# Rounding of the down weights moved from GpSimd to ScalarE, their stores to HBM set three pairs later in SyncE's order, the second layer's constants made in the second batch

## The chip, the cores and the metric

One core of one Trainium2 chip. The metric is the device time of one execution in microseconds, median of the runs.

## The reference

Two layers with residuals, x of shape (2, 1024, 256), all fp32:

```python
# layer 0: 8 experts and a shared one, F = 1024
g = einsum('bsd,edf->ebsf', h, Wg);  u = einsum('bsd,edf->ebsf', h, Wu)
expert_outs = einsum('ebsf,efd->ebsd', silu(g) * u, Wd)
expert_output = einsum('be,ebsd->bsd', gating_probs, expert_outs)
shared = (silu(h @ Sg) * (h @ Su)) @ Sd
x = x + (1 - sg) * expert_output + sg * shared
# layer 1: scores = tanh(x @ W1 + b1) @ v; per batch a mask (l<=j, l>=j or l!=j),
# p = softmax(where(mask, scores, -1e30)), x = x + (p @ x) / count(mask)
```

## The kernel before

**Work units.** The 9 experts (the shared one is the ninth) times 8 tiles of F give 72 *uses* of weights; two neighbouring uses are a *pair* (36 pairs). The groups i = 0 to 143 are batch 0's uses 0 to 71 and then batch 1's. Every fp32 matmul is made of three passes over a rounded part (hi) and a rest (lo), `three_pass`, L1477. Gate and up products use seven Strassen-like products per use instead of eight (`product`, L1482), so a use has 7 x 3 matmuls for gate and up and, in batch 0, 2 x 2 x 3 for the down product (`down`), each over 512 columns.

**Weights.** In batch 0 each weight is loaded raw, combined and split into hi and lo, used, and the split form is stored in HBM (`wq_kept` for gate and up, one use at a time; `wd_kept` for down, one pair at a time, with four sums of its tiles for batch 1). Batch 1 only fetches these.

- Gate/up of use n: GpSimd combines the raw tiles of a pair (`combine_pair`, L550 to L553), ScalarE rounds the hi (`round_w`, L792, issued three uses ahead), VectorE subtracts for the lo (`rest_w`, L1104). `wq` has three slots. `round_w(n)` waits until slot n % 3 is stored.
- Down of pair k: GpSimd does all: `split_d` (L564 adds zero to round, L567 subtracts), then `sums_d`: three sums (L580, L581, L582) in the raw buffer, their rounding (L584) and rest (L587). `raw_d` has two buffers, `wd` three slots.

**Order in each engine.** All orders are written out by hand. TensorE in use i (L1732 to L1764): p4(i), gate_start(i+1) (product 1), p5(i), down(0, i-2), gate_end(i+1) (product 2, which adds to what ScalarE's `seed` put down, and waits for it), p3(i), p7(i+1), p6(i+1), down(1, i-2). ScalarE in use i (L976 to L999): seed, gate_second, gate_first, round_h, keep_p7, round_h, keep_v, round_w; in uses 3 to 6 also batch 1's `round_x`. VectorE's loop L1369 to L1389 does batch 1's combinations and rests of x in uses 2 to 7.

SyncE issues all loads and stores of the loop in one order (L480 to L491):

```python
sp.wait_ge(gu_split, n + 1)
if n % PAIR == PAIR - 1 and m < NU // PAIR:
    load_gu(sp, m)
sp.dma_start(wq_kept[n], ...)
if n % PAIR == PAIR - 1:
    k = n // PAIR
    sp.wait_ge(td_split, k + 1)      # GpSimd's last rest of pair k, L587
    if m < NU // PAIR:
        load_d(sp, m)
    sp.dma_start(wd_kept[k], ...)
```

So the next use's store stands behind the last operation of GpSimd on the pair.

**Constants.** GpSimd makes the second layer's constants, flags and masks (63 small instructions, each waited for) between batch 0's uses: ahead of uses 13, 17, 21 and 25 (`EXTRA`, L669).

**Batch 1.** GpSimd has `sums_h(p)` alone (s3 L708, s1 L711, s2 L713, s4 L717), 35 times. ScalarE's odd group begins with `round_c("s3", p)`, which waits for L708, and has `seed` behind it. Batch 0's second layer is worked off in eight steps (`L1_STEP`) from group 74, two groups apart.

Of the kernel before, what the change touches and what calls it, by code (L numbers as in the profile page):

```python
# [6 lines left out]
F32 = mybir.dt.float32  # L7
# [25 lines left out]
def cond_resid_kernel(nc, x, fside, shared_gate, prompt_type, Wg, Wu, Wd, Sg, Su, Sd, W1, b1, v, out):  # L33
# [14 lines left out]
    RAWS = 2  # L48
    JB = BANK // D
# [20 lines left out]
    SPS = NU // PAIR - 1  # L70

# [6 lines left out]
    with ExitStack() as ctx:  # L78
# [52 lines left out]
        raw_d = place("raw_d", [P, RAWS, DN, P], F32, work_at + 8 * BANK * 4)  # L131
# [144 lines left out]
        staged_d = [sem(f"staged_d{s}") for s in range(RAWS)]  # L276
# [89 lines left out]
        L1_AT = end_of_b[0] + LAG + 1  # L366
# [81 lines left out]
        def load_d(queue, m):  # L448
            e, f = uses[m * PAIR]
            d = Wd[e] if e < E else Sd  # L450
            queue.dma_start(raw_d[:, m % RAWS, 0:PAIR * KD, :].rearrange("p (j k) d -> p j (k d)", k=KD),
                            d[f * P:(f + PAIR) * P, :].rearrange("(j p) d -> p j d", p=P)).then_inc(staged_d[m % RAWS], 16)
# [4 lines left out]
        @block.sync  # L457
        def _(sp):

            for i in range(0, NJ // PIECE, NT):  # L460
                load_x(sp, 0, i)
            load_x(sp, 0, NJ // PIECE - 1)
            load_w(sp, 0, Wg, (1,), slice(1, 3), staged_g[0])
            load_w(sp, 0, Wu, (1,), slice(0, 4, 3), staged_u[0])

            for i in range(NJ // PIECE):
                sp.wait_ge(x_loaded[0][i], 16)
            load_gu(sp, 1)
            sp.dma_start(probs[:], fside.unsqueeze(0).broadcast_to([P, B, E])).then_inc(gates_loaded, 16)
            sp.dma_start(sg[:], shared_gate.unsqueeze(0).broadcast_to([P, B])).then_inc(gates_loaded, 16)  # L470
            load_d(sp, 0)
            for i in range(NJ // PIECE):
                load_x(sp, 1, i)
            load_d(sp, 1)
            sp.dma_start(ptype_i[:], prompt_type.unsqueeze(0).broadcast_to([P, B])).then_inc(l1_loaded, 16)
            sp.dma_start(W1_sb[:, :, A:2 * A], W1.rearrange("(k p) a -> p k a", p=P)).then_inc(l1_loaded, 16)
            for t in range(NT):
                sp.dma_start(b1_sb[t * A:(t + 1) * A, :], b1.unsqueeze(1)).then_inc(l1_loaded, 16)
                sp.dma_start(v_sb[t * A:(t + 1) * A, t:t + 1], v.unsqueeze(1)).then_inc(l1_loaded, 16)
            for n in range(NU):  # L480
                m = n // PAIR + RAWS
                sp.wait_ge(gu_split, n + 1)
                if n % PAIR == PAIR - 1 and m < NU // PAIR:
                    load_gu(sp, m)
                sp.dma_start(wq_kept[n], wq[:, n % WR].bitcast(F32)).then_inc(wq_stored[n % WR], 16)
                if n % PAIR == PAIR - 1:
                    k = n // PAIR
                    sp.wait_ge(td_split, k + 1)
                    if m < NU // PAIR:
                        load_d(sp, m)  # L490
                    sp.dma_start(wd_kept[k], wd[:, k % DR].bitcast(F32)).then_inc(wd_stored[k % DR], 16)  # L491


            def fetch_d(p):

                k = SP0 + p
                if p < DR:
                    sp.wait_ge(wd_stored[k % DR], (SP0 - 1 - k % DR) // DR * 16 + 16)
                    sp.wait_ge(down_done[1], (k - DR + 1) * PAIR)
                else:  # L500
                    q = "s4" if (p - DR) % 2 else "a12"
                    sp.wait_ge(c_used[q], p - DR + 1)
                sp.dma_start(wd[:, k % DR].bitcast(F32), wd_kept[p]).then_inc(wd_fetched[k % DR], 16)

            for n in range(NU):
                i = NU + n
                sp.wait_ge(wq_stored[i % WR], (NU - 1 - i % WR) // WR * 16 + 16)
                sp.wait_ge(p_done[3], i - WR + 1)
                sp.dma_start(wq[:, i % WR].bitcast(F32), wq_kept[n]).then_inc(wq_fetched[i % WR], 16)
                if n % PAIR == 0 and n:  # L510
                    fetch_d(n // PAIR - 1)
            fetch_d(SPS)

            for b in range(B):
                for i in range(NJ // PIECE):
                    sp.wait_ge(out_done, b * NJ + (i + 1) * PIECE)
                    sp.dma_start(out_dram[b, i], x2[:, b, i * PIECE:(i + 1) * PIECE, :]).then_inc(stored, 16)
            sp.wait_ge(stored, 16 * B * NJ // PIECE)

        @block.gpsimd  # L520
        def _(pool):
# [33 lines left out]
            def split_d(n):  # L555
                s, j = n // PAIR % RAWS, n % PAIR
                if j == 0:
                    pool.wait_ge(staged_d[s], (n // PAIR // RAWS + 1) * 16)
                if n >= DR * PAIR:
                    pool.wait_ge(down_done[1], n - DR * PAIR + 1)  # L560
                    pool.wait_ge(wd_stored[n // PAIR % DR], n // PAIR // DR * 16)
                k, own = n // PAIR % DR, slice(j * KD, (j + 1) * KD)
                hi, lo = wd[:, k, 0, own, :], wd[:, k, 1, own, :]
                nc.gpsimd.tensor_tensor(hi, raw_d[:, s, own, :], zero[:, 0:1].unsqueeze(2).broadcast_to([P, KD, P]),  # L564
                                        ALU.add).then_inc(d_hi_done, 1)
                pool.wait_ge(d_hi_done, n + 1)
                nc.gpsimd.tensor_tensor(lo, raw_d[:, s, own, :], hi.bitcast(F32), ALU.subtract).then_inc(d_split, 1)  # L567
# [3 lines left out]
            def sums_d(k):  # L571


                def td_made(ins):
                    td_steps[0] += 1
                    ins.then_inc(td_step, 1)
                    pool.wait_ge(td_step, td_steps[0])

                w = raw_d[:, k % RAWS]
# [3 lines left out]
                hi, lo = wd[:, k % DR, 0, 4:DN, :], wd[:, k % DR, 1, 4:DN, :]  # L583
                nc.gpsimd.tensor_tensor(hi, w[:, 4:DN, :], zero[:, 0:1].unsqueeze(2).broadcast_to([P, DN - 4, P]),  # L584
                                        ALU.add).then_inc(td_hi_done, 1)
                pool.wait_ge(td_hi_done, k + 1)
                nc.gpsimd.tensor_tensor(lo, w[:, 4:DN, :], hi.bitcast(F32), ALU.subtract).then_inc(td_split, 1)  # L587
# [19 lines left out]
            def constants():  # L607
# [7 lines left out]
                const(nc.gpsimd.tensor_copy(to[:], to_i[:]))  # L615
                for at in LANES[1:]:
                    const(nc.gpsimd.tensor_scalar(lane[at:at + LANE, :], lane[at:at + LANE, :], -float(at), None, ALU.add))
                const(nc.gpsimd.tensor_scalar(lane_used[:], lane[:], float(NJ), None, ALU.is_lt))
                for m, compare in ((blk_before, ALU.is_gt), (blk_after, ALU.is_lt), (blk_same, ALU.is_equal)):
                    const(nc.gpsimd.tensor_scalar(m[:], to[:], lane[:, 0:1], lane_used[:, 0:1], compare, ALU.mult))  # L620
                const(nc.gpsimd.affine_select(out=eye[:], in_=ones[:, 0:NJ * NJ].rearrange("p (i j) -> p i j", j=NJ),
# [9 lines left out]
            def flags():  # L631
# [6 lines left out]
                const(nc.gpsimd.tensor_tensor(w_self[:], is_pre[:], is_post[:], ALU.add))  # L638
                for flag, w in ((f_before, w_before), (f_after, w_after), (f_self, w_self)):
# [5 lines left out]
            def masks(b):  # L645
# [7 lines left out]

                for m, one_way, other_way in ((blk_mask, blk_before, blk_after), (blk_mask_to, blk_after, blk_before)):
                    const(nc.gpsimd.tensor_scalar(m[:, b, :], one_way[:], w_before[:, one], None, ALU.mult))
                    const(nc.gpsimd.tensor_scalar(blk_part[:], other_way[:], w_after[:, one], None, ALU.mult))
                    const(nc.gpsimd.tensor_tensor(m[:, b, :], m[:, b, :], blk_part[:], ALU.add))
                for m in (mask[:, b, :], blk_mask[:, b, :], blk_mask_to[:, b, :]):
# [10 lines left out]
            EXTRA = {13: constants, 17: flags, 21: lambda: masks(0), 25: lambda: masks(1)}  # L669

            combine_pair(0)
            for n in range(NU):
                if n in EXTRA:
                    EXTRA[n]()
# [4 lines left out]
                split_d(n)  # L679
# [7 lines left out]
                if n == 3:  # L687
                    sums_d(0)
                if n % PAIR and n > 1:
                    sums_d(n // PAIR)  # L690
            assert steps[0] == CONST_STEPS
# [45 lines left out]
            for b in range(B):  # L737
# [3 lines left out]
                if b == 0:  # L741
                    for p in range(SPS):
                        sums_h(p)
                    join()
# [16 lines left out]
        def _(act):  # L761
# [21 lines left out]
            def round_w(n):  # L783

                act.wait_ge(t_step, 3 * (n // PAIR + 2 if n >= PAIR else n + 1))
                if n >= WR:
# [6 lines left out]
                                     ACT.Copy).then_inc(gu_hi_done, 1)  # L793

# [181 lines left out]
            for i in range(NU):  # L976
# [21 lines left out]
                for q in ROUND_X1.get(i, ()):  # L998
                    round_x(1, q)  # L999

# [62 lines left out]
        def _(dve):  # L1063
# [327 lines left out]
            def even(i, p):  # L1391
                second_gate(i)
                if i == L1_AT:
# [419 lines left out]
```

## Time and profile before

| | us |
|---|---|
| median of 3 runs | 1127.67 (1126.43 to 1129.34) |
| the profiled execution, its own time | 1127.99 |
| its span, first to last instruction | 1126.1 |
| TensorE busy in the span | 1104.9 (98%) |
| VectorE / ScalarE / GpSimd busy | 919.6 / 709.4 / 696.5 |

The profiled execution spends 1.9 us around its span. Batch 0's half ends at about 560 us. A sum of gains and losses is made against 1127.99, and what it gives is to be compared with the median of 1127.67, which is 0.3 us less.

### The profile page before, as it was taken

How to read it: one execution, taken by the hardware profiler on the slowest of the kernel's cores; microseconds unless marked ns; L12 is line 12 of the kernel's file. 1: busy time of each engine (PE TensorE's matmuls, PEld its weight loads, DVE VectorE, ACT ScalarE, POOL GpSimd, SP SyncE). 2: the span in 40 equal slices, each digit the busy share in tenths (PEclk: the TensorE clock that was granted, in tenths of full speed). 3: DMA queues.
4: the chain of work that ended last, by engine and by line, in shares of the span. 5: the costliest groups of instructions: out<-in, count | busy, mean ns of one | idle time of the engine just before them, and what ended most of it. 6: DMA issues, size and time to landing. Idle time of an engine off the chain costs nothing. (4 is left out here: it accounts for less than half of the span.)

```text
span 1126.1 us, 16076 instructions
## 1 busy us (share of the span) xinstructions
PE 1104.9 (98%) x4856; PEld 903.9 (80%) x4856; DVE 919.6 (82%) x1218; ACT 709.4 (63%) x1268; POOL 696.5 (62%) x666
## 2 busy tenths in 40 slices
PE   8799999999999999999999999999999999999988
PEld 6577888778888888888878887888888888888866
DVE  6698777788877877787668899888888898888875
ACT  6475666566666666666556666666666666666663
POOL 7799999999987777778324444444444444444451
PEclk9899999999999999999999999999999999999999
DMA  6666665487666666666545555555555555555512
GB/s 218 251 259 233 249 231 212 177 306 283 235 259 262 261 237 235 239 233 255 218 173 203 179 198 182 203 204 203 206 206 206 206 206 205 206 205 206 203 41 75
DMA packets 66484, 241.24 MB, mean 214 GB/s; under 512 B 6496, under 2 KB 38752, under 8 KB 57184
## 3 DMA queue, kind: packets, MB, share of 16 engines
q1 hardware_dynamic: 65584, 239.70, 57.6%
q8 instruction: 40, 0.66, 0.2%
q10 hardware_dynamic: 816, 0.52, 0.2%
q14 instruction: 44, 0.36, 0.1%
HBM read 134.29 MB, written 105.91 MB: 213 GB/s over the span
## 5 line engine op out<-in xcount | busy, mean ns | idle before, releaser
L811 ACT ACTIVATE silu<-g_ps 128x512 f32<-128x512 f32 x144 | 86.3, 599 | 180.1 <-PE g_ps L1480 180.1
L1478 PE MATMUL v_both<-xs_hi,wq 128*128 128x512 f32 x432 | 170.0, 393 | 3.3 <-DVE up L1146 2.6
L1479 PE MATMUL v_both<-xs_hi,wq 128*128 128x512 f32 x432 | 168.6, 390 | 0.0
L1480 PE MATMUL v_both<-xs_lo,wq 128*128 128x512 f32 x432 | 168.5, 390 | 0.0
L1141 DVE TENSOR_TENSOR gate<-e_ps,v_part 128x512 f32<-128x512 f32 x144 | 99.0, 687 | 66.4 <-PE e_ps L1480 66.2
L805 ACT ACTIVATE v_both<-g_ps 128x512 f32<-128x512 f32 x144 | 83.9, 583 | 101.7 <-PE g_ps L1480 101.4
L711 POOL TENSOR_TENSOR a<-a,a_own 128x512 f32<-128x512 f32 x35 | 56.1, 1604 | 137.4 <-DVE a_own L1173 137.4
L708 POOL TENSOR_TENSOR s<-a_own,a 128x512 f32<-128x512 f32 x35 | 56.3, 1610 | 131.0 <-DVE a_own L1192 131.0
L1478 PE MATMUL g_ps<-xs_hi,wq 128*128 128x512 f32 x288 | 113.0, 392 | 9.5 <-ACT v_both L805 9.5
L817 ACT ACTIVATE p_sb<-e_ps 128x512 f32<-128x512 f32 x144 | 86.2, 598 | 48.4 <-PE e_ps L1480 47.5
L1478 PE MATMUL e_ps<-xs_hi,wq 128*128 128x512 f32 x288 | 112.7, 391 | 0.4 <-ACT p_sb L817 0.4
L1480 PE MATMUL g_ps<-xs_lo,wq 128*128 128x512 f32 x288 | 112.4, 390 | 0.0
L1479 PE MATMUL e_ps<-xs_hi,wq 128*128 128x512 f32 x288 | 112.3, 390 | 0.0
L1480 PE MATMUL e_ps<-xs_lo,wq 128*128 128x512 f32 x288 | 112.3, 390 | 0.0
L1479 PE MATMUL g_ps<-xs_hi,wq 128*128 128x512 f32 x288 | 112.3, 390 | 0.0
L1478 PE MATMUL acc_of<-h_hi,wd 128*128 128x512 f32 x288 | 112.0, 389 | 0.0
L1479 PE MATMUL acc_of<-h_hi,wd 128*128 128x512 f32 x288 | 112.0, 389 | 0.0
L1480 PE MATMUL acc_of<-h_lo,wd 128*128 128x512 f32 x288 | 112.0, 389 | 0.0
L1146 DVE TENSOR_TENSOR up<-v_both,p_sb 128x512 f32<-128x512 f32 x144 | 98.7, 685 | 7.2 <-PE v_both L1480 3.3
L1104 DVE TENSOR_TENSOR wq<-raw,wq 128x896 fp32r<-128x896 f32 (+1 forms) x70 | 94.3, 1347 | 10.9 <-ACT wq L792 10.9
L1478 PEld LDWEIGHTS v_both<-xs_hi,wq 128*128 128x128 f32 x432 | 81.3, 188 | 24.9 <-DVE up L1146 7.3
L1201 DVE TENSOR_TENSOR a_lo<-a_own,a_hi 128x512 fp32r<-128x512 f32 x72 | 84.0, 1167 | 15.4 <-ACT a_hi L865 15.4
(233 smaller groups left out, 2883.5 us busy)
## 6 DMA issues: line engine op xcount, KB each, us to landing
wq_kept<-wq SPq DMA_DIRECT2D x72, 896.0 KB, 5.5
wq<-wq_kept SPq DMA_DIRECT2D x72, 896.0 KB, 4.5
wd_kept<-wd SPq DMA_DIRECT2D x36, 1024.0 KB, 5.4
wd<-wd_kept SPq DMA_DIRECT2D x36, 1024.0 KB, 6.1
raw_d<-in_L_cond_Wd SPq DMA_DIRECT2D x32, 256.0 KB, 3.1
raw<-in_L_cond_Wg SPq DMA_DIRECT2D x31, 256.0 KB, 2.7
raw<-in_L_cond_Wu SPq DMA_DIRECT2D x31, 256.0 KB, 3.5
out_x<-x SPq DMA_DIRECT2D x8, 256.0 KB, 2.1
```

The lines of the kernel that those rows point to most:

```text
L708: nc.gpsimd.tensor_tensor(s3[:], a_own[:], a21[p % 2][:], ALU.subtract).then_inc(sum_made["s3"], 1)
L711: nc.gpsimd.tensor_tensor(a21[p % 2][:], a21[p % 2][:], a_own[:], ALU.add).then_inc(sum_made["s1"], 1)
L805: nc.scalar.activation(v_ps[i % 2][:], g_ps[:], ACT.Copy).then_inc(seeded, 1)
L811: nc.scalar.activation(silu0[:, i % 2, :], g_ps[:], ACT.Silu).then_inc(silu0_done, 1)
L817: nc.scalar.activation(p7_sb[:], e_ps[:], ACT.Copy).then_inc(p7_copied, 1)
L1104: nc.vector.tensor_tensor(lo[:, part, :], raw[:, s, 1 + part.start:8, j * P:(j + 1) * P], hi[:, part, :].bitcast(F32), ALU.subtract).then_ ...
L1141: nc.vector.tensor_tensor(gate1[:], e_ps[:], v_part[:], ALU.add).then_inc(gate1_done, 1)
L1146: nc.vector.tensor_tensor(up1[:], v_ps[i % 2][:], p7_sb[:], ALU.add).then_inc(up1_done, 1)
L1201: nc.vector.tensor_tensor(lo, src[:], hi.bitcast(F32), ALU.subtract).then_inc(c_split[q], 1)
L1478: nc.tensor.matmul(ps, w_hi, a_hi, start=start, stop=False, skip_group_check=True)
L1479: nc.tensor.matmul(ps, w_lo, a_hi, start=False, stop=False, skip_group_check=True)
L1480: return nc.tensor.matmul(ps, w_hi, a_lo, start=False, stop=stop, skip_group_check=True)
```

## The change

Four things. (1) The hi parts of the down weights of pairs 1 to 35 are rounded by ScalarE (`round_d` at the end of even uses) and not by GpSimd; the hi parts of the sums of all pairs too (`round_td` at the end of odd uses). GpSimd keeps the subtractions (`rest_d`, `rest_td`) and the sums. (2) SyncE waits for `td_split` of pair k, loads down weights of pair k+3 and stores pair k only at use 2(k+3) (`KEEP = 3`); the last three pairs are stored between batch 1's first fetches. (3) `raw_d` has three buffers. (4) The constants are made in nine kinds of pieces after `sums_h(p)`, p = 1 to 11, and batch 0's second layer begins at group 104 in place of 74 (`L1_AT = NU + 32`).

```diff
+    RAWD = 3
+    KEEP = 3
-        L1_AT = end_of_b[0] + LAG + 1
+        ADD_AT = end_of_b[0] + LAG + 1
+        L1_AT = NU + 32
@@ SyncE
+            def keep_d(k):
+                sp.wait_ge(td_split, k + 1)
+                if k + RAWD < NU // PAIR:
+                    load_d(sp, k + RAWD)
+                sp.dma_start(wd_kept[k], wd[:, k % DR].bitcast(F32)).then_inc(wd_stored[k % DR], 16)
             for n in range(NU):
                 ...
-                if n % PAIR == PAIR - 1:
-                    k = n // PAIR
-                    sp.wait_ge(td_split, k + 1)
-                    if m < NU // PAIR:
-                        load_d(sp, m)
-                    sp.dma_start(wd_kept[k], ...)
+                if n == 1:
+                    load_d(sp, 2)
+                if n % PAIR == 0 and n // PAIR >= KEEP:
+                    keep_d(n // PAIR - KEEP)
             for n in range(NU):          # batch 1's fetches
+                k = (NU + n) // PAIR - KEEP
+                if n % PAIR == 0 and k < NU // PAIR:
+                    keep_d(k)
@@ GpSimd
+            def rest_d(k):
+                pool.wait_ge(d_hi_done, PAIR + k)
+                nc.gpsimd.tensor_tensor(wd[:, k % DR, 1, own, :], raw_d[k % RAWD][:, own, :],
+                                        wd[:, k % DR, 0, own, :].bitcast(F32), ALU.subtract)
+            def rest_td(k):
+                pool.wait_ge(td_hi_done, k + 1)
+                nc.gpsimd.tensor_tensor(... 4:DN ... subtract).then_inc(td_split, 1)
-            EXTRA = {13: constants, 17: flags, 21: lambda: masks(0), 25: lambda: masks(1)}
             combine_pair(0)
             for n in range(NU):
                 if n % PAIR == 0 and n + PAIR < NU:
                     combine_pair(n // PAIR + 1)
-                split_d(n)
-                if n % PAIR and n > 1:
-                    sums_d(n // PAIR)
+                if n < PAIR:
+                    split_d(n)
+                k = n // PAIR - 1
+                if n % PAIR == 0:
+                    if k >= 1:
+                        rest_d(k)
+                        rest_td(k - 1)
+                elif k >= 0:
+                    sums_d(k)
@@ GpSimd, batch 1, after sums_h(p)
+  p in 1..11: wait s4; edges, lanes, blanks, flags, biases, mask_of(0), block_masks(0),
+              mask_ends(0), mask_of(1), block_masks(1), mask_ends(1)
@@ ScalarE
+            def round_d(k):
+                act.wait_ge(staged_d[k % RAWD], (k // RAWD + 1) * 16)
+                if k >= DR:
+                    act.wait_ge(down_done[1], (k - DR + 1) * PAIR)
+                    act.wait_ge(wd_stored[k % DR], k // DR * 16)
+                nc.scalar.activation(wd[:, k % DR, 0, own, :], raw_d[k % RAWD][:, own, :], ACT.Copy)
+            def round_td(k):
+                act.wait_ge(td_step, 3 * (k + 1))
+                nc.scalar.activation(wd[:, k % DR, 0, 4:DN, :], raw_d[k % RAWD][:, 4:DN, :], ACT.Copy)
             for i in range(NU):
                 ...
+                if i % PAIR:
+                    round_td(i // PAIR)
+                elif i:
+                    round_d(i // PAIR)
```

## Rows read from the trace of the kernel before

**Rows 1.** Windows: busy us (count) of PE, PEld, DVE, ACT, POOL, then clock and DMA.

```profile
60.00:92.00 32.00, 30.65 (x133) 24.30 (x133) 31.44 (x37) 21.55 (x37) 30.36 (x28) 1.00 0.70 265
800.00:1060.00 260.00, 260.00 (x1149) 215.29 (x1148) 232.44 (x311) 171.63 (x311) 113.80 (x74) 1.00 0.56 201
```

**Rows 2.** Waits of TensorE: total us, times, longest.

```profile
PE g_ps L1478 <- ACT v_both L805: 9.5, 3, 7.8
PE v_both L1478 <- DVE up L1146: 2.6, 5, 0.8
```

**Rows 3.** Timeline of TensorE at 38 to 52 us: start, duration, [idle before].

```profile
38.53 0.39 PE L1480 MATMUL acc_of<-h_lo,wd 128*128 128x512 f32 x1
46.70 0.80 PE L1478 MATMUL g_ps<-xs_hi,wq 128*128 128x512 f32 x1 [7.78 <-ACT v_both L805]
51.86 0.39 PE L1478 MATMUL acc_of<-h_hi,wd 128*128 128x512 f32 x1
```

**Rows 4.** Timeline of TensorE at 223 to 229 us.

```profile
223.31 0.39 PE L1480 MATMUL acc_of<-h_lo,wd 128*128 128x512 f32 x1
225.17 0.50 PE L1478 MATMUL g_ps<-xs_hi,wq 128*128 128x512 f32 x1 [1.48 <-ACT v_both L805]
228.92 0.39 PE L1478 MATMUL acc_of<-h_hi,wd 128*128 128x512 f32 x1
```

**Rows 5.** Timeline of ScalarE: what stood before both gaps, and a regular seed.

```profile
45.21 0.95 ACT L792 ACTIVATE wq<-raw 128x896 fp32r<-128x896 f32 x1 [10.05 <-DMA wq_kept<-wq]
...
223.69 0.95 ACT L792 ACTIVATE wq<-raw 128x896 fp32r<-128x896 f32 x1 [3.82 <-POOL raw L553]
...
539.19 0.58 ACT L805 ACTIVATE v_both<-g_ps 128x512 f32<-128x512 f32 x1 [0.98 <-PE g_ps L1480]
```

**Rows 6.** Waits of SyncE's queue in the first 100 us.

```profile
SPq L451 <- POOL wd L587: 39.0, 4, 17.0
```

**Rows 7.** Timeline of SyncE's queue, first 60 us.

```profile
38.10 0.43 SPq L485 DMA_DIRECT2D wq_kept<-wq  x1
```

**Rows 8.** Groups of GpSimd, by form: busy us, mean ns, idle before.

```profile
L587 POOL TENSOR_TENSOR wd<-raw_d,wd 128x512 fp32r<-128x512 f32 x36 | 63.9, 1774 | 2.8
L584 POOL TENSOR_TENSOR wd<-raw_d,zero 128x512 fp32r<-128x512 f32 x36 | 42.0, 1167 | 2.8
L580 POOL TENSOR_TENSOR raw_d<-raw_d 128x256 f32<-128x256 f32 x36 | 35.2, 978 | 0.0
L581 POOL TENSOR_TENSOR raw_d<-raw_d 128x128 f32<-128x128 f32 x36 | 21.9, 607 | 2.8
L582 POOL TENSOR_TENSOR raw_d<-raw_d 128x128 f32<-128x128 f32 x36 | 20.9, 579 | 2.8
```

**Rows 9.** Groups of ScalarE, by form: a rounding from SBUF.

```profile
L835 ACT ACTIVATE h_hi<-h 128x512 fp32r<-128x512 f32 x72 | 45.2, 627 | 7.9 <-DVE h L1173 7.2
```

**Rows 10.** Groups of VectorE, by form: rests in batch 1's half.

```profile
L1201 DVE TENSOR_TENSOR a_lo<-a_own,a_hi 128x512 fp32r<-128x512 f32 x72 | 84.0, 1167 | 15.4 <-ACT a_hi L865 15.4
L1201 DVE TENSOR_TENSOR s_lo<-a,s_hi 128x512 fp32r<-128x512 f32 x71 | 48.5, 684 | 0.0
```

**Rows 11.** Timeline of GpSimd: first and last row of one mask's first six instructions.

```profile
204.24 0.78 POOL L647 TENSOR_SCALAR cnt<-pos,cnt_slope,cnt_rest 128x8 f32<-128x8 f32 x1
...
208.49 0.47 POOL L652 TENSOR_TENSOR mask<-mask,mask_part 128x128 f32<-128x128 f32 x1
```

**Rows 12.** Timeline of GpSimd, ScalarE and TensorE in a regular odd group of batch 1.

```profile
767.28 1.62 POOL L708 TENSOR_TENSOR s<-a_own,a 128x512 f32<-128x512 f32 x1 [3.44 <-DVE a_own L1192]
769.00 0.63 ACT L865 ACTIVATE s_hi<-s 128x512 fp32r<-128x512 f32 x1 [0.36 <-POOL s L708]
770.43 0.58 ACT L805 ACTIVATE v_both<-g_ps 128x512 f32<-128x512 f32 x1 [0.80 <-PE g_ps L1480]
771.59 0.39 PE L1478 MATMUL g_ps<-xs_hi,wq 128*128 128x512 f32 x1
```

More of the change, by code:

```diff
@@ L130, in cond_resid_kernel @@
         raw = place("raw", [P, RAWS, 8, PAIR * P], F32, work_at)
-        raw_d = place("raw_d", [P, RAWS, DN, P], F32, work_at + 8 * BANK * 4)
+        raw_d = [place(f"raw_d{n}", [P, DN, P], F32, work_at + at * BANK * 4) for n, at in enumerate((8, 10, 25))]
         blank = place("blank", [P, BANK], F32R, work_at + 12 * BANK * 4)
@@ L275, in cond_resid_kernel @@
         first_u = sem("first_u")
-        staged_d = [sem(f"staged_d{s}") for s in range(RAWS)]
+        staged_d = [sem(f"staged_d{s}") for s in range(RAWD)]
         wq_stored = [sem(f"wq_stored{s}") for s in range(WR)]
@@ L450, in load_d @@
             d = Wd[e] if e < E else Sd
-            queue.dma_start(raw_d[:, m % RAWS, 0:PAIR * KD, :].rearrange("p (j k) d -> p j (k d)", k=KD),
-                            d[f * P:(f + PAIR) * P, :].rearrange("(j p) d -> p j d", p=P)).then_inc(staged_d[m % RAWS], 16)
+            queue.dma_start(raw_d[m % RAWD][:, 0:PAIR * KD, :].rearrange("p (j k) d -> p j (k d)", k=KD),
+                            d[f * P:(f + PAIR) * P, :].rearrange("(j p) d -> p j d", p=P)).then_inc(staged_d[m % RAWD], 16)
         def load_x(queue, b, i):
@@ L485, in _ @@
                 sp.dma_start(wq_kept[n], wq[:, n % WR].bitcast(F32)).then_inc(wq_stored[n % WR], 16)
-                if n % PAIR == PAIR - 1:
-                    k = n // PAIR
-                    sp.wait_ge(td_split, k + 1)
-                    if m < NU // PAIR:
-                        load_d(sp, m)
-                    sp.dma_start(wd_kept[k], wd[:, k % DR].bitcast(F32)).then_inc(wd_stored[k % DR], 16)
+                if n == 1:
+                    load_d(sp, 2)
+                if n % PAIR == 0 and n // PAIR >= KEEP:
+                    keep_d(n // PAIR - KEEP)
             def fetch_d(p):
@@ L506, in _ @@
                 i = NU + n
+                k = i // PAIR - KEEP
+                if n % PAIR == 0 and k < NU // PAIR:
+                    keep_d(k)
                 sp.wait_ge(wq_stored[i % WR], (NU - 1 - i % WR) // WR * 16 + 16)
@@ L555, in split_d @@
             def split_d(n):
[L556 to L564, printed above, removed]
+                if n == 0:
+                    pool.wait_ge(staged_d[0], 16)
+                own = slice(n * KD, (n + 1) * KD)
+                hi, lo = wd[:, 0, 0, own, :], wd[:, 0, 1, own, :]
+                nc.gpsimd.tensor_tensor(hi, raw_d[0][:, own, :], zero[:, 0:1].unsqueeze(2).broadcast_to([P, KD, P]),
                                         ALU.add).then_inc(d_hi_done, 1)
                 pool.wait_ge(d_hi_done, n + 1)
-                nc.gpsimd.tensor_tensor(lo, raw_d[:, s, own, :], hi.bitcast(F32), ALU.subtract).then_inc(d_split, 1)
+                nc.gpsimd.tensor_tensor(lo, raw_d[0][:, own, :], hi.bitcast(F32), ALU.subtract).then_inc(d_split, 1)
+            def rest_d(k):
+                own = slice(0, PAIR * KD)
+                pool.wait_ge(d_hi_done, PAIR + k)
+                nc.gpsimd.tensor_tensor(wd[:, k % DR, 1, own, :], raw_d[k % RAWD][:, own, :],
+                                        wd[:, k % DR, 0, own, :].bitcast(F32), ALU.subtract).then_inc(d_split, PAIR)
             td_steps = [0]
@@ L577, in td_made @@
                     pool.wait_ge(td_step, td_steps[0])
-                w = raw_d[:, k % RAWS]
+                w = raw_d[k % RAWD]
                 td_made(nc.gpsimd.tensor_tensor(w[:, 4:6, :], w[:, 1:4:2, :], w[:, 0:2, :], ALU.subtract))
@@ L582, in sums_d @@
                 td_made(nc.gpsimd.tensor_tensor(w[:, 7, :], w[:, 2, :], w[:, 6, :], ALU.subtract))
-                hi, lo = wd[:, k % DR, 0, 4:DN, :], wd[:, k % DR, 1, 4:DN, :]
-                nc.gpsimd.tensor_tensor(hi, w[:, 4:DN, :], zero[:, 0:1].unsqueeze(2).broadcast_to([P, DN - 4, P]),
-                                        ALU.add).then_inc(td_hi_done, 1)
+            def rest_td(k):
                 pool.wait_ge(td_hi_done, k + 1)
-                nc.gpsimd.tensor_tensor(lo, w[:, 4:DN, :], hi.bitcast(F32), ALU.subtract).then_inc(td_split, 1)
+                nc.gpsimd.tensor_tensor(wd[:, k % DR, 1, 4:DN, :], raw_d[k % RAWD][:, 4:DN, :],
+                                        wd[:, k % DR, 0, 4:DN, :].bitcast(F32), ALU.subtract).then_inc(td_split, 1)
             def combine_pair(m):
@@ L605, in combine_pair, with edges @@
                 combine(s, slice(P, PAIR * P))
-            def constants():
+            def edges():
                 for m, sign in ((before, 1), (after, -1)):
@@ L615, in constants, with lanes @@
                 const(nc.gpsimd.tensor_copy(to[:], to_i[:]))
+            def lanes():
                 for at in LANES[1:]:
@@ L620, in constants, with blanks @@
                     const(nc.gpsimd.tensor_scalar(m[:], to[:], lane[:, 0:1], lane_used[:, 0:1], compare, ALU.mult))
+            def blanks():
                 const(nc.gpsimd.affine_select(out=eye[:], in_=ones[:, 0:NJ * NJ].rearrange("p (i j) -> p i j", j=NJ),
@@ L638, in flags, with biases @@
                 const(nc.gpsimd.tensor_tensor(w_self[:], is_pre[:], is_post[:], ALU.add))
+            def biases():
                 for flag, w in ((f_before, w_before), (f_after, w_after), (f_self, w_self)):
@@ L643, in flags, with mask_of @@
                 const(nc.gpsimd.tensor_tensor(cnt_rest[:], cnt_rest[:], w_self[:], ALU.add))
-            def masks(b):
+            def mask_of(b):
                 one = slice(b, b + 1)
@@ L652, in masks, with block_masks @@
                     const(nc.gpsimd.tensor_tensor(mask[:, b, :], mask[:, b, :], mask_part[:], ALU.add))
+            def block_masks(b):
+                one = slice(b, b + 1)
                 for m, one_way, other_way in ((blk_mask, blk_before, blk_after), (blk_mask_to, blk_after, blk_before)):
@@ L657, in masks, with mask_ends @@
                     const(nc.gpsimd.tensor_tensor(m[:, b, :], m[:, b, :], blk_part[:], ALU.add))
+            def mask_ends(b):
                 for m in (mask[:, b, :], blk_mask[:, b, :], blk_mask_to[:, b, :]):
@@ L667, in make_gates @@
                                         ALU.mult).then_inc(gate_step, 1)
-            EXTRA = {13: constants, 17: flags, 21: lambda: masks(0), 25: lambda: masks(1)}
             combine_pair(0)
             for n in range(NU):
-                if n in EXTRA:
-                    EXTRA[n]()
                 if n % PAIR == 0 and n + PAIR < NU:
@@ L686, in _ @@
                     nc.gpsimd.tensor_tensor(lo[:], raw[:, 1, 1:8, 0:P], hi[:].bitcast(F32), ALU.subtract).then_inc(gu_split, 1)
-                if n == 3:
-                    sums_d(0)
-                if n % PAIR and n > 1:
-                    sums_d(n // PAIR)
-            assert steps[0] == CONST_STEPS
+                k = n // PAIR - 1
+                if n % PAIR == 0:
+                    if k >= 1:
+                        rest_d(k)
+                    if k >= 1:
+                        rest_td(k - 1)
+                elif k >= 0:
+                    sums_d(k)
+            last = NU // PAIR - 1
+            rest_d(last)
+            rest_td(last - 1)
+            sums_d(last)
+            rest_td(last)
             def rest_carry(b, n):
@@ L743, in _ @@
                         sums_h(p)
+                        if p in range(1, 12):
+                            pool.wait_ge(sum_made["s4"], p + 1)
+                        if p == 1:
+                            edges()
+                        elif p == 2:
+                            lanes()
+                        elif p == 3:
+                            blanks()
+                        elif p == 4:
+                            flags()
+                        elif p == 5:
+                            biases()
+                        elif p in (6, 9):
+                            mask_of(p // 8)
+                        elif p in (7, 10):
+                            block_masks(p // 8)
+                        elif p in (8, 11):
+                            mask_ends(p // 11)
+                    assert steps[0] == CONST_STEPS
                     join()
@@ L793, in round_w @@
                                      ACT.Copy).then_inc(gu_hi_done, 1)
+            def round_d(k):
[3 more added lines that the diff above has]
+                    act.wait_ge(wd_stored[k % DR], k // DR * 16)
+                own = slice(0, PAIR * KD)
+                nc.scalar.activation(wd[:, k % DR, 0, own, :], raw_d[k % RAWD][:, own, :], ACT.Copy).then_inc(d_hi_done, 1)
+            def round_td(k):
+                act.wait_ge(td_step, 3 * (k + 1))
+                nc.scalar.activation(wd[:, k % DR, 0, 4:DN, :], raw_d[k % RAWD][:, 4:DN, :],
+                                     ACT.Copy).then_inc(td_hi_done, 1)
             def seed(i):
@@ L1392, in even @@
                 second_gate(i)
-                if i == L1_AT:
+                if i == ADD_AT:
                     add_acc(1, end_of_b[0])
```

## The prediction

> **What bounds the kernel now.** I read the windows first. TensorE has no gap in long stretches: 260.00 us busy of 260, with 1149 matmuls, so one takes 0.2263 us and a use of 33 matmuls 7.47 us [rows 1]. So a gain can only come from a gap or from slow matmuls, and less work on another engine is worth nothing by itself. Next, TensorE's waits. Besides the start and the tail there are two kinds: for ScalarE's seed, 9.5 us in three waits with one of 7.8, and for VectorE's `up`, 2.6 us in five [rows 2].
>
> Then the timeline at the two places. The long wait is followed by slow matmuls. In the code, twelve matmuls lie between the first one after the gap and the first one at normal pace, so from 38.53 to 51.86 us are 13 steps: 13 x 0.2263 = 2.94 us of work took 13.33 [rows 3]. The loss is 10.39 us: 7.9 idle and the rest from matmuls up to 0.80 us long, at the clock after the gap. At 223 us the same 13 steps took 5.61 us [rows 4]: loss 2.67.
>
> What made them? Ahead of the late seed stands `round_w`. The first waited 10.05 us for a store of `wq` [rows 5], issued only at 38.10 [rows 7]. In SyncE's order that store (use 2) stands behind the wait for GpSimd's last rest of pair 0, and SyncE's queue spent 39.0 us in four such waits, up to 17.0 each [rows 6]. The second `round_w` waited 3.82 us for GpSimd's own combination [rows 5], just after GpSimd had made a mask (rows of [rows 11] lie 15 us earlier). Both gaps are thus GpSimd being late, once through SyncE's order and once directly.
>
> **The change part by part.**
>
> *SyncE's order.* Store 2 no longer stands behind pair 0: it needs `gu_split` 3 only, which GpSimd gives in its first use. Store 3, the loads of pair 3 and all later ones move forward likewise; `load_d(2)` goes out at use 1. Each `keep_d(k)` asks for `td_split` of a pair three behind, which GpSimd ends about two uses earlier, so SyncE doesn't stand still in it, and what is queued behind it (load of down pair k+3, store of pair k, next `wq` stores) isn't late. The bytes are the same. Gain: 10.39 us.
>
> *GpSimd in batch 0.* It loses the rounding adds (1167 ns per pair at L584 and two of half size at L564) [rows 8] and all constants. That work is on no path of TensorE's by itself, but it is the lateness behind the second gap. Gain: 2.67 us. Cover gone would mean both gaps back, 13.06 us.
>
> *ScalarE in batch 0.* One more rounding of 128x512 per use: 0.63 us by the nearest row [rows 9]. It stands between `round_w` and the next seed, where ScalarE idles 0.98 us [rows 5]. How late may a seed be? The second gap tells: ScalarE was held 3.82 us and TensorE came 225.17 - 223.31 - 0.23 = 1.63 us late, so 2.2 us were absorbed. Cost in steady state 0.
>
> *Its waits.* `round_d(k)` waits for a load, a store and a down product; all were asked for well over a use before. `round_td(k)` waits for GpSimd's sums, and behind it stand seed, gates and TensorE. The chain from the end of `round_d(k)`: `rest_d` 1.77 (a 128x512 rest, like L587), `rest_td(k-1)` 1.77, sums 0.98 + 0.61 + 0.58 [rows 8], five hand-offs of 2.8/36 = 0.08: 6.1 us. `round_td(k)` is due one use after `round_d(k)` began: 7.47 - 0.63 = 6.8 us. Room 0.7, and 2.2 more before TensorE notices. Cost 0; lower bound 0; upper bound, if a chain in the first uses is late by a microsecond beyond that room, 1 each for two or three.
>
> *Third raw buffer, last three stores.* They only loosen waits; the fetches of batch 1 stand behind `keep_d(33)` to `keep_d(35)`, whose waits end before the fetch could go. Cost 0.
>
> *Uses 2 to 7.* Here VectorE has batch 1's x as well: 31.44 us busy of 32, TensorE 30.65 [rows 1]. The long gap let VectorE rest ahead of it. Without it, use 3 meets the same limit, so I add one more wait for `up` of the size of the others, with its slower first matmul: 0.8 us (bounds 0 and 2).
>
> *Constants in batch 1.* They lie in GpSimd's idle time between s4 and the next s3, 3.44 us [rows 12]. The longest piece is `mask_of`: 204.24 to 208.96, 4.7 us [rows 11], with the hand-offs 1.4 late. Then ScalarE rounds s3 at 770.4 instead of 769.00, seed starts 770.95 instead of 770.43 and ends 0.5 us later, at about 771.5; TensorE wants it at 771.59 [rows 12]. That is just in time, twice. A slower piece comes through one to one. VectorE can also be held up: a rest that meets GpSimd takes 1167 ns, one that doesn't 684 [rows 10]. I take 0.8 us for all eleven pieces, from below 0, from above 12 (rival D).
>
> The Trainium skill (SBUF — State Buffer, Who interferes with whom) says that a VectorE instruction with two SBUF inputs and a GpSimd one that reads SBUF exclude each other for the whole instruction, while ScalarE waits for nobody. This speaks for moving the rounding and against the new place of the constants; the pair 1167 and 684 ns agrees. By that rule the sum would stay as it is or go to rival D's.
>
> *Second layer at group 104.* Same work, same eight steps; the groups around it look the same. Cost 0.
>
> **Sum.** 1127.99 - 10.39 - 2.67 + 0.8 + 0.8 = 1116.5 us. The profiled execution is 0.3 above the median; I leave that in the range.
>
> **The rivals.**
>
> *A, as summed*: both gaps go. Its own range 1113.5 to 1119.5: bounds of the `up` waits (some of today's could shrink too, as GpSimd does less beside VectorE: 2.6 us at most) and 0 to 3 for the constants.
>
> *B, a part comes back*: ScalarE, VectorE and GpSimd are all near their limit in uses 1 to 8, and without the gap no one catches up. A late `round_td` or `rest_w` opens a new gap of 2 to 5 us, with slow matmuls behind it as in [rows 3]. For it: 31.44 of 32. Against it: 2.2 us of room for a seed. 1119.5 to 1123; I write 1121.
>
> *C, the first gap stays*: something besides the order holds `wq`'s store, as the DMA queues themselves. Against it: the row names the store, and it went out at 38.10. Only 2.67 gained: 1125.3.
>
> *D, no gain by contention in batch 1*: 63 instructions of GpSimd are put beside VectorE. If each lengthens one VectorE instruction by 1167 - 684 = 0.48 us, that is 30 us; VectorE idles 27.6 us of 260 [rows 1], some 1.6 per pair, so 11 pairs absorb 18 and 12 reach TensorE: 1128.5, that is no change. The rule quoted above would let this happen. Against it: most of the 63 are tiny, and they wait in turn.
>
> *E, slower*: the ScalarE and GpSimd chain. It is 6.1 us and may be 6.8 + 2.2 = 9.0. If contention stretches each GpSimd instruction by half, it is 9.2, which costs 0.2 us per pair, 7 us in 36, and only eats part of the gain. It decides against the change from 9.0 + 11.5/36 = 9.3 us on; at 9.5 us it is 36 x 0.5 = 18 us, so 1134.5. Against it: the 1774 ns of `L587` already hold today's contention.
>
> **How the numbers follow.** A 0.73, B 0.15, C 0.03, D 0.05, E 0.04. A change under 0.3% (3.4 us) is about what can't be told from none. A and B are faster, and a little of C and D: 0.90. Same 0.06, slower 0.04. The predicted time is A's. The range takes A and most of B: 1112.5 to 1121.5.
>
> **What would show it.** In the profile after: SyncE's `wq` store of use 2 goes out near 22 us, and its queue has no long wait for GpSimd; TensorE's wait of 7.8 us is gone and the granted clock stays full from 36 to 60 us; batch 1 begins about 13 us earlier. Per pair ScalarE has two 128x512 roundings into `wd`, and GpSimd's idle time before `rest_d` is filled with a wait for ScalarE. Around 610 to 730 us GpSimd's idle time before L708 shrinks, at `mask_of` to zero. Wrong would be: TensorE waiting for a seed behind `round_td` in each pair (E), new waits at 25 to 90 us (B), or `up` waits in batch 1's first third (D).

## The result and the profile after

The changed kernel takes 1122.72 us (median of 4 runs, 1122.43 to 1123.38), the kernel before 1128.2 in the same comparison. The ratio is 0.9954, with a 95% interval from 0.9936 to 0.9971: 5.5 us faster. The forecast was 1116.5, more than twice that gain, and the time lies above the upper end of the range (1121.5). The profiled execution took 1122.43 us with a span of 1120.7, against 1127.99 and 1126.1.

What was forecast of both gaps is there. In the waits of SyncE's queue in the first 100 us no line names GpSimd's last rest any more ([rows 6] had 39.0 us of it). The store of use 2 goes out at 22.01 us and not at 38.10 [rows 7]. These are the two with the largest totals, and a line of the queue's timeline:

```profile
SPq L445 <- DVE wq L1176: 30.7, 6, 7.6
SPq L498 <- DVE wq L1176: 27.9, 5, 7.4
```

```profile
22.01 0.34 SPq L498 DMA_DIRECT2D wq_kept<-wq  x1
```

The waits of TensorE's matmuls over the whole span leave nothing to explain a missing 6 us. These are the two with the largest totals; the first is the tail's:

```profile
PE acc_of L1550 <- issue: 2.4, 1, 2.4
PE v_both L1550 <- DVE up L1218: 1.9, 4, 0.6
```

The windows show it. These three rows are the same stretch of the kernel before, of the changed one and of experiment e1 (below), with the busy time of TensorE first and its count of matmuls in brackets:

```profile
60.00:560.00 500.00, 496.57 (x2182) 408.31 (x2182) 393.51 (x471) 311.79 (x533) 417.48 (x456) 1.00 0.64 245
```

```profile
60.00:560.00 500.00, 498.96 (x2171) 404.54 (x2170) 388.87 (x465) 342.00 (x593) 299.18 (x258) 1.00 0.65 242
```

```profile
60.00:560.00 500.00, 499.68 (x2203) 413.39 (x2202) 385.58 (x470) 349.52 (x599) 281.93 (x262) 1.00 0.66 246
```

TensorE is *busier* than before and does *fewer* matmuls in the 500 us: 2171 against 2182, although a gap was taken out. A matmul's row covers about 0.39 us while the next starts after 0.23, so a delay of up to 0.16 us is no idle time in the rows of the matmuls. One list of waits does name it, that of TensorE's weight loads (PEld). At 95 to 560 us, first before, then after:

```profile
PEld v_both L1478 <- DVE up L1146: 2.5, 8, 1.0
PEld v_both L1550 <- DVE up L1218: 9.9, 30, 0.3
```

Thirty waits in some 62 uses are one per pair. Their sum is what the weight loads waited, not what TensorE lost; for that I look at spacings, and take the start of ScalarE's `silu<-gate` of each use. In the changed kernel:

```profile
388.25 0.62 ACT L897 ACTIVATE silu<-gate 128x512 f32<-128x512 f32 x1
395.97 0.62 ACT L897 ACTIVATE silu<-gate 128x512 f32<-128x512 f32 x1
403.45 0.62 ACT L897 ACTIVATE silu<-gate 128x512 f32<-128x512 f32 x1
411.13 0.62 ACT L897 ACTIVATE silu<-gate 128x512 f32<-128x512 f32 x1
```

The distances are 7.72, 7.48, 7.68. I count a distance for the use or group in which it ends (the last of these is use 52's). Every use that should take 7.48 us does so when it is odd, and takes 7.68 to 7.73 when it is even. From use 10 to 70 this sums to 6.9 us. The same reading over both kernels gives the ledger of the difference (the changed kernel's lead over the kernel before, at the start of `silu<-gate` of that group):

| at group | lead, us | what lies between |
|---|---|---|
| 9 | 10.3 | first gap gone, uses 2 to 8 |
| 25 | 8.6 | eight even uses |
| 26 | 11.3 | second gap gone |
| 71 | 6.9 | even uses, less what before lost itself (about 13 was forecast here) |
| 104 | 15.2 | before has done the second layer of batch 0 here |
| 120 | 6.8 | the changed kernel does it here |
| 143 | 6.8 | |
| end of span | 5.4 | the tail |

The last step is new too. Both kernels wait some 2.4 us ahead of the last pair. In the changed one TensorE's clock then falls. Windows of the stretch behind that wait, first of before, then of after (the granted clock is the third number from the end):

```profile
1090.50:1094.50 4.00, 3.96 (x17) 3.10 (x18) 2.84 (x3) 3.99 (x13) 3.78 (x4) 1.00 0.02 4
```

```profile
1083.50:1087.50 4.00, 3.72 (x9) 3.00 (x10) 3.06 (x4) 3.99 (x12) 3.54 (x4) 0.57 0.01 4
```

Nine matmuls start there in place of 17, at a mean granted clock of 0.57: most of the stretch is at the lower of its two levels, 1.2 GHz.

### The profile page after: what moved, and what is told of

Its sections match the earlier page's. It is cut to its first block and busy times, and to the rows that moved or that the text cites. A ratio compares the mean times of both kernels' runs of the same rounds, so it can differ in the third digit from the quotient of the medians.

```text
span 1120.7 us, 15976 instructions
## 1 busy us (share of the span) xinstructions
PE 1109.0 (99%) x4856; PEld 901.3 (80%) x4856; DVE 921.3 (82%) x1218; ACT 746.8 (67%) x1339; POOL 603.5 (54%) x525
## 5 line engine op out<-in xcount | busy, mean ns | idle before, releaser
L584 POOL TENSOR_TENSOR wd<-raw_d,wd 128x512 fp32r<-128x512 f32 x35 | 46.3, 1324 | 190.8 <-ACT wd L855 190.8
L1176 DVE TENSOR_TENSOR wq<-raw,wq 128x896 fp32r<-128x896 f32 (+1 forms) x70 | 108.6, 1552 | 0.0
```

The costliest lines, as they stand in the source:

```text
L584: nc.gpsimd.tensor_tensor(wd[:, k % DR, 1, own, :], raw_d[k % RAWD][:, own, :], wd[:, k % DR, 0, own, :].bitcast(F32), ALU.subtract).then_ ...
L1176: nc.vector.tensor_tensor(lo[:, part, :], raw[:, s, 1 + part.start:8, j * P:(j + 1) * P], hi[:, part, :].bitcast(F32), ALU.subtract).then_ ...
```

## The experiments

**Who makes even uses slow.** Three timelines of the changed kernel around 403 us, first VectorE's, then GpSimd's, then TensorE's:

```profile
402.89 2.00 DVE L1176 TENSOR_TENSOR wq<-raw,wq 128x896 fp32r<-128x896 f32 x1
404.82 0.68 DVE L1218 TENSOR_TENSOR up<-v_both,p_sb 128x512 f32<-128x512 f32 x1
```

```profile
402.66 1.29 POOL L584 TENSOR_TENSOR wd<-raw_d,wd 128x512 fp32r<-128x512 f32 x1 [5.51 <-ACT wd L855]
403.89 2.15 POOL L604 TENSOR_TENSOR wd<-raw_d,wd 128x512 fp32r<-128x512 f32 x1
```

```profile
405.25 0.39 PE L1552 MATMUL g_ps<-xs_lo,wq 128*128 128x512 f32 x1
405.55 0.50 PE L1550 MATMUL v_both<-xs_hi,wq 128*128 128x512 f32 x1
405.89 0.40 PE L1551 MATMUL v_both<-xs_hi,wq 128*128 128x512 f32 x1
```

ScalarE's `round_d` ends (L855) and releases `rest_d` at 402.66, 0.23 us before VectorE's `rest_w` starts. This takes 2.00 us; `up` behind it is late, and TensorE's p3 starts 0.30 us after its predecessor, with a first step of 0.34. Both are 0.23 normally. The theory T is that these two instructions meet once in every pair, and that this makes the distance up to the even use longer. The rival R1 is that ScalarE's added rounding does it.

*e1: the two kept apart.*

```diff
             def rest_d(k):
                 pool.wait_ge(d_hi_done, PAIR + k)
+                if PAIR * k + 3 < NU:
+                    pool.wait_ge(gu_split, PAIR * k + 4)
```

> The changed kernel, but GpSimd's rest_d(k) also waits for VectorE's rest_w of use 2k+3 (gu_split 2k+4), so the two no longer run side by side; ScalarE's work and order are untouched. Theory T (in every even use of batch 0 rest_w, 2.0 us beside rest_d, makes VectorE's up late and TensorE loses 0.2 us): ScalarE's silu<-gate again follows itself at 7.48 us in even uses, rest_w falls to about 1.2 us in them, 33 x 0.2 = 7 us gained on the changed kernel's 1122.7: about 1116 (1114.5 to 1118). Rival R1 (ScalarE's added rounding in front of the seed costs the 0.2): unchanged, 1122 to 1124. Rival R2 (delaying rest_d makes the chain to round_td late): slower than 1123.

Measured 1113.47 us (1113.28 to 1115.09), ratio to before 0.9874 (0.9861 to 0.9888): 9.2 us less than the changed kernel. All uses from 10 to 71 take 7.48 us. A line on one source line (count, then shortest, median and longest ns) for `rest_w` at 95 to 560 us, first in the changed kernel, then in e1:

```profile
L1176 DVE TENSOR_TENSOR wq<-raw,wq x59: 1082/2003/2009, 99.3 to 539.5; 128x896 fp32r<-128x896 f32 x59
```

```profile
L1178 DVE TENSOR_TENSOR wq<-raw,wq x59: 1081/1084/1419, 98.0 to 531.8; 128x896 fp32r<-128x896 f32 x59
```

T holds and the rivals fall: ScalarE does the same work, and one more wait on GpSimd makes the kernel faster. By the profiled executions it is 8.9 us, of which 7.5 are there at group 143: 1.0 by use 9 and 6.9 in the even uses, less 0.4 at groups 93 and 94. The other 1.4 are the tail's clock, below. The time is below the range given for T, which had neither the tail nor the first uses in it. In the other use of each pair `rest_w` takes 1.41 us in e1, beside GpSimd's combination, and this costs nothing.

*e2: the subtractions replaced by memsets.*

```diff
-                nc.gpsimd.tensor_tensor(wd[..., 1, own, :], raw_d[...], wd[..., 0, own, :], ALU.subtract)
+                nc.gpsimd.memset(wd[:, k % DR, 1, own, :].bitcast(F32), 0.0)
                 # and the same in rest_td
```

> The changed kernel with rest_d and rest_td as memsets: the lo parts of the down weights of pairs 1 to 35 and of all their sums are left out (zero), so GpSimd reads nothing there and is quicker. ScalarE's work, its waits and all transfers stay. T: no 0.2 us per even use, about 1116, rest_w of even uses under 1.4 us. R1 (ScalarE) or R3 (the transfers' traffic): even uses stay at 7.68, 1122 to 1124.

Measured 1113.96 us. Uses from 10 on take 7.48 us, and `rest_w` 1163 ns in the mean. In the even uses it runs beside two memsets, which stand where the subtractions stood (VectorE's timeline, then GpSimd's):

```profile
397.09 1.08 DVE L1174 TENSOR_TENSOR wq<-raw,wq 128x896 fp32r<-128x896 f32 x1
```

```profile
396.84 0.53 POOL L584 MEMSET wd<- 128x512 f32 x1 [7.01 <-ACT wd L853]
397.30 0.53 POOL L603 MEMSET wd<- 128x512 f32 x1
```

This too ends R1, and the rival that the transfers do it (all of them are there): the delay needs GpSimd's subtractions at that moment. The memsets don't read, and they are shorter as well (0.53 us); but `rest_w` isn't even delayed to the end of the memset that was running when it began. The Trainium skill (SBUF — State Buffer, Who interferes with whom) has the lock that fits: a VectorE instruction with two SBUF inputs and a GpSimd one that reads SBUF, not one that only writes it, meet in it, and the second to issue waits for the whole of the first. The trace agrees within 0.15 us: at 402.89 `rest_w` had 1.06 us to wait for the end of `rest_d` and took 0.92 longer than alone, and GpSimd's next subtraction ended 1.15 us after `rest_w`, where one of this size takes 1.29 undisturbed.

*e3: the rounding back on GpSimd.* `split_d` and `sums_d` as in the kernel before (with three raw buffers), ScalarE without `round_d` and `round_td`; order and constants as changed.

> The changed kernel with the rounding back on GpSimd (new SyncE order, three raw buffers and constants in batch 1 are kept; ScalarE has nothing added). T: GpSimd's operations are no longer tied to ScalarE's round_d and fall on rest_w in no fixed place; both gaps of before stay away, so 1128.2 - 13 + 1 = about 1116 (1114 to 1118). If instead the new place of stores and loads, or any collision with GpSimd, costs the 0.2 us per even use, it stays at 1122 or above.

Measured 1121.1 us: the forecast missed by 5. The start is one cause. Without the first gap GpSimd, with 12 us of work per pair and a late begin, falls behind in uses 3 to 5 (10.79 and 9.28 us for two of them), and `silu<-gate` of use 9 is 5.3 us behind e1's. The other: GpSimd is tied again, to the store of `wd`, and lengthens *odd* uses by 0.04 to 0.13 us, 2.3 us in all; `rest_w` takes some 1.85 us there, once per pair. Lines of its waits, GpSimd's at 100 to 540 us and ScalarE's at 20 to 60:

```profile
POOL wd L578 <- DMA wd_kept<-wd: 78.1, 29, 4.4
```

```profile
ACT wq L831 <- POOL raw L567: 3.4, 1, 3.4
```

So moving the rounding to ScalarE is worth 5.3 + 2.3 us where `rest_d` is kept off `rest_w` (e1). Where it isn't, as in the changed kernel, it is worth nothing: 1122.7 against e3's 1121.1 by the medians, 1122.4 against 1122.3 in the profiled executions, which both have the low clock in the tail.

*e4: SyncE's order, with the third raw buffer and the later second layer.* As e3, constants back ahead of uses 13, 17, 21 and 25. These three are not told apart.

> As e3, and the constants back ahead of uses 13, 17, 21 and 25 of batch 0: of the change only SyncE's order, the third raw buffer and the later second layer are left. T: the first gap is gone (10.1 us), and a gap of up to 3 us may be left behind the masks: 1117 to 1119.5. Rival: with three buffers and the later stores GpSimd has more run-ahead, the second gap is gone too, and it equals e3.

Measured 1128.04 us, ratio 1.0 (0.9991 to 1.0009). The order takes 6.5 us out by use 9 and most of it is given back: gaps at uses 22, 23 and 26 behind the masks (11.41, 8.46 and 9.91 us for 7.48, 7.3 in all, against 2.9 in the kernel before), and the small delays of e3. In the profiled execution, the fastest of ten, 1.9 us are left; the medians show nothing. At 160 to 240 us ScalarE's `round_w` waited twice for GpSimd's combination, up to 4.9 us:

```profile
ACT wq L830 <- POOL raw L567: 8.3, 2, 4.9
```

I read it so: with the gap gone, TensorE reaches the masks sooner, and GpSimd's lateness, which the gap had covered, is seen there.

*e5: only the constants back in batch 0*, with ScalarE rounding.

> The changed kernel with the constants, flags and masks back ahead of uses 13, 17, 21 and 25 of batch 0; ScalarE's rounding and SyncE's order stay. Theory: GpSimd has some 5.5 us of idle time per pair there, but its place is tied to ScalarE's round_d; the 8 to 9 us of constants and of each mask come in front of a combination or a rest, are late by 3 to 4 us, of which about 2.9 us are absorbed: gaps of 0.5 to 3 us three times. Against it, 0.4 us less in batch 1 (groups 87 and 93): 1124 to 1128. Rival: GpSimd's idle time hides all of them: 1122.3, and the move of the constants was worth nothing with the rounding on ScalarE.

Measured 1143.41 us, ratio 1.0142 (1.0128 to 1.0155): 20.7 us over the changed kernel. The sign was right, the size four times the most that I gave (5.3). The four blocks cost 6.0 + 1.7, 3.2 less 1.1, 7.3 and 7.4 us. GpSimd's timeline at the first block (its first and last instruction), and then ScalarE's:

```profile
102.36 0.74 POOL L627 TENSOR_SCALAR_AFFINE_SELECT before<-ones 128x128 f32<-128x128 f32 x1
...
110.14 0.19 POOL L651 CAST pos<-pos_i 128x8 f32<-128x8 int32 x1
```

```profile
112.23 0.63 ACT L859 ACTIVATE wd<-raw_d 128x512 fp32r<-128x512 f32 x1 [6.23 <-POOL raw_d L600]
```

The 8 us stand between `rest_td` and the sums that `round_td` waits for, so nearly all of them are late, and GpSimd's idle time of 5.5 us comes after, not before. Rival E of the prediction, the ScalarE and GpSimd chain, is real as soon as anything is put into it. The move of the constants isn't a matter of 2.7 us: it is worth 6.9 us with the rounding on GpSimd (e4 to e3) and 20.7 with it on ScalarE.

**The tail.** *e6: matmuls in the wait.*

```diff
                 k, done = SP0 + SPS, {}
+                for _ in range(8):
+                    nc.tensor.matmul(e_ps[:], xs_hi[1][:, 0, 0:P], xs_hi[1][:, 0, :], start=True, stop=True, ...)
```

> The changed kernel with eight matmuls of 128x512 (their result is read by nobody) in TensorE's wait of 2.35 us ahead of the last pair. Theory: the profile of the changed kernel has 8 matmuls at 0.43 us behind this wait (the clock fell), as before has not; with TensorE busy the clock stays, 8 x 0.2 = 1.4 us gained: 1121.3. The fillers are 1.8 us and end before the wait does. Rival: the low clock there was this one execution's only, and the median stays at 1122.7, or is later by the part of the fillers that doesn't fit.

Measured 1121.35 us (1120.77 to 1121.54), 1.4 below, as forecast. From group 143 to the end of the span e6 takes 41.4 us and the changed kernel 42.8, so the gain is where it should be. TensorE's timeline of e6 has the fillers in the wait, and the last pair at full pace:

```profile
1081.58 1.98 PE L1645 MATMUL e_ps<-xs_hi 128*128 128x512 f32 x8
1084.12 0.47 PE L1550 MATMUL acc_of<-a_hi,wd 128*128 128x512 f32 x1 [0.57 <-issue]
1084.43 0.40 PE L1551 MATMUL acc_of<-a_hi,wd 128*128 128x512 f32 x1
```

*e7: e1 with the fillers.*

> e1_rest_after_rest_w with the same eight matmuls as in e6. Its profiled execution ran the last pair at full clock, but its four times lie between 1113.28 and 1115.09. Theory: the scatter is the tail's clock; with the fillers all lie at 1113.3 or 0.3 below, none above 1114. Rival: no effect on median or spread.

Measured 1113.49 us (1113.10 to 1113.92), none above 1114, though not all within 0.3 of 1113.3. The median is e1's: by its mean granted clock (0.998 and not 1.000) e1 had the low clock in one of its four times only, 1115.09. That the fillers narrow the scatter agrees with the theory but four times are few.

**The order's distance.** *e8: e1 with `KEEP = 2`.*

> e1_rest_after_rest_w with KEEP = 2: each down pair is stored and the next raw pair loaded one pair earlier in SyncE's order. Theory: at its place td_split of that pair comes about half a use after SyncE gets there (GpSimd ends rest_td(k) behind rest_d(k+1)), so SyncE stands for some microseconds per pair and what is behind it (the store of the next wq, the next gate and up load) goes out later; wq's stores have over a use of slack, so 1113.5 to 1115. Rival: the order of before was bad only because of uses 0 to 3, and at KEEP = 2 the start has a gap again: 1116 or more.

Measured 1126.71 us, outside the theory's range. For batch 0 the theory held: the late stores cost nothing (use 70 is reached 0.95 us earlier than in e1). The start has no gap, so the rival's reason is wrong as well. The loss is at the transition, which neither named. ScalarE's timeline, SyncE's queue there, and TensorE's wait at 540 to 575 us:

```profile
555.97 0.58 ACT L875 ACTIVATE v_both<-g_ps 128x512 f32<-128x512 f32 x1 [11.39 <-PE g_ps L1554]
```

```profile
547.26 0.32 SPq L491 DMA_DIRECT2D wd_kept<-wd  x1
547.69 1.34 SPq L523 DMA_DIRECT2D wq<-wq_kept  x2
```

```profile
PE g_ps L1552 <- DMA wq<-wq_kept: 10.5, 2, 9.1
```

With `KEEP = 2` the store of pair 34, which waits for GpSimd, stands ahead of batch 1's first fetch of `wq`; that goes out only at 547.69, and TensorE waits for it.

*e9: the same, the last two stores at e1's places.*

```diff
+    KEEP = 2
+                if n in (2, 4):
+                    keep_d(NU // PAIR - 3 + n // 2)
```

> e8 lost its time in one place: after use 70 ScalarE's silu<-gate is 17.56 us behind the last instead of 7.48, since keep_d(34) stood in front of batch 1's first fetch of wq. Here KEEP = 2 in batch 0's loop, and the last two pairs are stored where e1 stores them, ahead of the fetches of uses 74 and 76. Theory: that gap (some 12.9 us with what follows it) is gone, and what e8 had gained over e1 by use 70 (0.95 us) stays: 1112.6 (1112 to 1113.5). Rival: KEEP = 2 leaves SyncE so late at the transition that a part comes back: 1114 to 1120.

Measured 1113.53 us (1112.91 to 1115.34), just above the theory's range. The gap at the transition is gone, 13 us, but no more than e1 came of it: e8's lead over e1 in use 9 was 0.96 us, e9's is 0.43 and turns into -0.4 by use 23. `KEEP` 2 or 3 makes no difference that these runs can tell.

*e10: e9 with the fillers, and `mask_of` in two pieces.*

> e9 with the fillers of e6 and with mask_of cut in two pieces of some 2.4 us, after p = 6 and 7 and after p = 10 and 11, so that GpSimd has ended each before the next s3 is due. Theory: groups 87 and 93 (8.23 and 8.26 us in e1 for 7.48, of which the next group gave back half) lose nothing: 0.8 us less than e9, 1111.8, and no run above 1112.5. Rival: more GpSimd pieces collide with VectorE in other groups and it equals e9.

Measured 1112.94 us (1112.03 to 1113.17), ratio to before 0.9862 (0.9847 to 0.9876). Groups 87 and 93 take 7.44 and 7.48 us, and group 143 comes 1.1 us earlier than in e9, with a start 0.35 us later. Of the 1.1 us, 0.8 come after group 72, as the theory had it for the masks. By medians e10 is 0.6 below e9, and 1.1 above the 1111.8 that I gave; three of its four times are above 1112.5. It beats both kernels. Its four times are all below e1's four, but the intervals of the ratios overlap, so I don't call it faster than e1.

## Why the prediction was wrong

*The two gaps (-10.39 and -2.67).* Right. The lead at use 9 is 10.3 us, with the cost of uses 2 to 7 in it (-10.39 + 0.8 was forecast), and the second gap gives 11.3 - 8.6 = 2.7. That SyncE's order *alone* would bring the first of them, as the part on it says with "Gain: 10.39", is wrong: e4 has 6.5 us by use 9, and 1.9 at the end of its profiled execution, 0.1 by the medians.

*The step that failed: "Cost in steady state 0" for the rounding on ScalarE.* I weighed ScalarE's queue (0.98 us idle before the seed, 2.2 us of room) and the chain to `round_td`, and both held: e1 and e2 leave ScalarE's work as it is. In the changed kernel's timeline the seed still has 0.47 us of idle before it, and GpSimd waits for ScalarE, not ScalarE for GpSimd:

```profile
POOL wd L584 <- ACT wd L855: 190.8, 35, 9.2
```

What I didn't ask is *when* `rest_d` would now run. A wait on ScalarE's `round_d` fixes its start to a point in TensorE's cycle, and 0.2 us later `rest_w` starts there, with `up` and p3 behind it. Before, GpSimd ran free and met `rest_w` at any phase; its median there was 1275 ns, and TensorE's weight loads waited for `up` 8 times and not 30 in the same stretch. The cost was 6.9 us in 31 even uses. I had the mechanism in hand, with its rule, and applied it to the constants in batch 1 (rival D) only; my text even read it as "speaks for moving the rounding".

*Constants in batch 1 (+0.8).* Small, as forecast, and half of it. `mask_of` makes groups 87 and 93 late by 0.8 and 0.25 us, and the next group gives back 0.42 and 0.25: 0.4 in all. GpSimd's timeline of the first, and the s3 that it pushes:

```profile
662.70 0.35 POOL L671 TENSOR_SCALAR cnt<-pos,cnt_slope,cnt_rest 128x8 f32<-128x8 f32 x1
...
668.01 1.29 POOL L742 TENSOR_TENSOR s<-a_own,a 128x512 f32<-128x512 f32 x1
```

5.3 us for the six instructions, where 4.7 was read from [rows 11]. (The pieces are of eight kinds, not nine: three of them are made once for each mask.) Rival D didn't happen. But the constants' other side was missed: "that work is on no path of TensorE's by itself" holds only at the new place (e5).

*The second layer at group 104 (0).* Right to 0.3 us: it costs 8.4 us here (15.2 to 6.8). At its old place it cost 8.7: the lead grows by 8.3 there, with the constants' 0.4 taken off.

*The tail.* Not in the sum. +1.4 us, shown by e6. A low clock behind [rows 3]'s gap was read, but a second wait of the same kind, of 2.4 us and untouched by the change, I took as fixed. Whether the change brought the low clock or chance did, the runs don't say.

*The sum again:* 1127.99 - 10.3 - 2.7 + 6.1 (6.88 in the even uses, less 0.74 that the kernel before lost in its own uses from 9 to 71, its second gap left out) + 0.4 (constants) - 0.3 (second layer) + 1.4 (tail) = 1122.6. Measured 1122.43.

*Rivals.* B named the right size (1121) and range for the wrong place: nothing new opens in uses 1 to 8. E's chain isn't late here; e5 shows what happens if it is. That E speaks of "0.2 us per pair, 7 us in 36", the very size that was lost, is chance: its way there is a late chain, and it puts that case inside the gain.

*Open.* Why the clock falls behind the last wait in some executions and not in others. With the same 2.4 us of waiting it fell in the profiles of the changed kernel, e2, e3, e5 and e9, and not in those of before, e1, e4 and e8. It is not a matter of the kernel alone: e1's own four times seem to differ by it. Nor did any run show which of GpSimd's inputs matters, or what the third raw buffer is worth by itself.

## What to carry to other kernels

A wait that ties one engine's instruction to another engine's fixes *when* it runs. Ask which instruction of a third engine starts at that point, not only whether the queue behind the wait has room; VectorE and GpSimd subtractions on SBUF are such a pair, and a wait that makes GpSimd later can be the cure. When busy time says 100%, count instructions per stretch or take the spacing of one instruction per iteration: a delay of 0.2 us that comes back 31 times is no idle time of the matmuls. Look also at what the weight loads waited for: here that list named `up`, once per pair.

## What the runs showed of the hardware

- A VectorE subtraction of 128x896 on SBUF took 1.08 us alone and 2.00 beside two GpSimd subtractions of 128x512. The second of these took 2.15 us, against 1.75 in e1; the first took 1.29 in both.
- Beside two GpSimd memsets of 128x512 (e2) it took 1.08 us; its mean over both uses of a pair was 1163 ns.
- After a wait of 2.35 us ahead of the last pair the granted clock was 0.57 over the next 4 us in one profile (changed kernel) and 1.00 in another (before, 2.36 us). With eight matmuls of 128x512 in the wait it was 1.00 in all three kernels that had them (e6, e7, e10).
